# Graph layers computed as A(xW) in place of (Ax)W, in a one-core graph, mixer and FFN block

## The reference

```
xn = layernorm(x)
g  = prelu(xn @ lin_W.T + lin_b)
for l in 0, 1:
    h = g + segment_sum(g[src], dst)                  # = A g, A = I + counts of edges
    h = prelu(h @ W1[l].T + b1[l], conv_a[l])
    h = h @ W2[l].T + b2[l]
    g = relu(batchnorm_over_nodes(h))
m  = linear attention mixer of xn (q softmax over 64, k softmax over nodes), projected, layernormed
x  = x + g + m
x  = x + ffn(layernorm(x))                            # weights merged from 8 experts by a gate
```

## Time and profile before

| what | value |
|---|---|
| median of 3 runs | 558.52 us |
| profiled execution | 561.2 us, of which 558.6 us from first to last instruction |
| busy | PE 496.5 us (89%), DVE 342.3 (61%), ACT 233.5 (42%), POOL 165.5 (30%) |
| chain that ended last | PE 65%, DVE 19%, ACT 7%, issue 5% |
| granted clock of PE, mean | 0.954 of full speed |

### The profile page before, as it was taken

The page is one execution under the profiler, slowest core; times in us unless marked ns, Lnnn a source line. Parts: engine busy times, 40 slices in busy tenths (PEclk is TensorE's granted clock), DMA queues, the critical chain, the costliest instruction groups (busy, mean ns, idle before and its releaser), DMA issues.

```text
span 558.6 us, 11588 instructions
## 1 busy us (share of the span) xinstructions
PE 496.5 (89%) x3909; PEld 389.9 (70%) x3909; DVE 342.3 (61%) x731; ACT 233.5 (42%) x533; POOL 165.5 (30%) x142
## 2 busy tenths in 40 slices
PE   2988599999889889999999988799999978989792
PEld 2776488766455756679988877599888857856541
DVE  4679888589798267555266543212675375537686
ACT  4744122553323422224255448211355377733343
POOL 1564400040860300024974610000446023304312
PEclk9998799999999899999999997899999957999997
DMA  8502200020200200020000010000210294000014
GB/s 247 164 2 75 76 1 3 1 75 1 77 0 1 78 1 1 1 79 0 0 1 0 11 66 1 3 1 0 82 48 0 79 412 191 2 0 2 0 54 129
DMA packets 5246, 27.45 MB, mean 49 GB/s; under 512 B 1036, under 2 KB 1161, under 8 KB 3544
## 3 DMA queue, kind: packets, MB, share of 16 engines
q1 hardware_dynamic: 5208, 26.92, 13.9%
HBM read 24.36 MB, written 2.56 MB: 48 GB/s over the span
## 4 chain that ended last, share of the span: by engine, by line
PE 65%; DVE 19%; ACT 7%; issue 5%; POOL 1%; DVEq 1%; DMA 1%; ACTq 0%; SPq 0%
PE ps L455 38%; PE ps L600 15%; PE ps L442 4%; PE ps L509 3%; PE ps L499 2%; DVE stage L1447 2%; DVE ohs L1078 1%; DVE r L1159 1%; DVE r L1087 1%; DVE late L1088 1%; PE ps L709 1%; PE ps L439 1%; ACT r L920 1%; DVE r L1517 1%; ACT late L837 1%
## 5 line engine op out<-in xcount | busy, mean ns | idle before, releaser
L455 PE MATMUL ps<-late,wslot 128*128 x960 | 104.7, 269 | 1.0 <-ACT ohs L894 0.9
L455 PE MATMUL ps<-r,wslot 128*128 128x250 f16 x840 | 99.8, 279 | 5.1 <-DVE r L1087 5.0
L455 PEld LDWEIGHTS ps<-late,wslot 128*128 128x128 f16 x960 | 92.3, 97 | 13.1 <-issue 3.5
L1578 POOL TENSOR_TENSOR wslot<-stage,wslot 128x2048 f16<-128x2048 f32 x9 | 36.8, 4086 | 206.4 <-ACT wslot L752 129.0
L455 PEld LDWEIGHTS ps<-r,wslot 128*128 128x128 f16 x840 | 84.3, 101 | 18.5 <-DVE r L1087 6.6
L600 PE MATMUL ps<-late,r 125*128 (+1 forms) x800 | 90.5, 274 | 4.9 <-issue 3.4
L600 PEld LDWEIGHTS ps<-late,r 125*128 125x128 f16 x800 | 78.6, 99 | 15.1 <-issue 6.0
L455 PE MATMUL ps<-wslot,r 128*125 128x512 f16 x300 | 71.3, 387 | 2.6 <-DVE late L1088 2.6
L1088 DVE SCALAR_TENSOR_TENSOR late<-ps,late 128x250 f32 (+2 forms) x60 | 29.1, 502 | 61.2 <-ACT late L927 55.6
L455 PEld LDWEIGHTS ps<-wslot,r 128*125 128x125 f16 (+1 forms) x300 | 39.5, 138 | 26.5 <-DVE late L1088 4.0
L759 ACT ACTIVATE late<-ps 125x500 f16<-125x500 f32 (+1 forms) x25 | 14.7, 588 | 100.6 <-PE ps L442 100.6
(11 more groups left out here) (174 smaller groups left out, 697.2 us busy)
## 6 DMA issues: line engine op xcount, KB each, us to landing
late<-in_tv SPq DMA_DIRECT2D x2, 4096.0 KB, 17.4
x<-in_x SPq DMA_DIRECT2D x5, 448.0 KB
out<-r SPq DMA_DIRECT2D x10, 224.0 KB
stage<-in_w_up SPq DMA_DIRECT2D x2, 1024.0 KB, 5.1
stage<-in_w_down SPq DMA_DIRECT2D x2, 1024.0 KB, 4.9
stage<-in_w_lin SPq DMA_DIRECT2D x1, 1024.0 KB, 6.8
stage<-in_w_k SPq DMA_DIRECT2D x1, 1024.0 KB, 6.1
stage<-in_w_q SPq DMA_DIRECT2D x1, 1024.0 KB, 4.7
```

Source lines behind the costliest of these rows:

```text
L455: last = nc.tensor.matmul(out, stat_(hs, b), mov(hm, b), start=start and n == 0, stop=stop and n == 3 * blocks - 1)
L1578: nc.gpsimd.tensor_tensor(wslot[:, i % SLOTS, 1].rearrange("p k n -> p (k n)"), stage[:, :], wslot[:, i % SLOTS, 0].rearrange("p k n -> p ...
```

## The change

Since A(g W1) = (A g) W1, the first weight is applied before the gather. A natural product ("up0", "up1": `up_tile`) with the transposed features `in_t` as stationary operand gives u = g W1 in rows, which is what the gather takes as its stationary operand. So:

- the 80 flips of features to rows (`x0`, `x1`) and the transposed products up0 and up1 go; 10 natural tiles of 12 matmuls with 512 columns come in for each layer: those of layer 0 between the linear and the key stage, those of layer 1 in the ramp in which the flips were;
- the PSUM of the gather is taken up with the bias and goes straight to the PReLU; `high_sums` and `low_sums` go; the high and low parts of the features are made before the product (layer 0: `high_in`, `low_in` in the linear stage; layer 1: `high_in1` with the ReLU on ACT, `low_in1` on DVE);
- windows: one for each of the tiles 5 to 9 of up0, one a chunk in the key stage, the value stage as before, one for each of the first five mixer tiles; the check of the counts is moved into the last mixer tiles and `first_sums` goes; DVE loads five window columns at a time;
- weights: ACT scales them and writes the high part, POOL only the low part, and DVE's high parts go, but for lin and up0, which DVE and ACT make in the linear stage;
- the mixer's layernorm on ACT and POOL is spread over gather 0 and down0; loops of ACT, DVE and POOL there are unrolled; buffers change places (`gnn_t` in r2, x2 in r3, index preparation in `late`).

The core of the diff:

```diff
-WEIGHTS = ["lin", "k", "q", "v", "out", "up0", "down0", "up1", "down1", "gate"]
+WEIGHTS = ["lin", "up0", "k", "q", "v", "out", "down0", "up1", "down1", "gate"]
-WINDOWS = {"k": 2, "v": 2, "mix": 1}
+WINDOWS = {"up0": 1, "k": 1, "v": 2, "mix": 1}
+UP_LAG, FIRSTS_AT = 5, 2
 # PE
+            def up_tile(layer, t):
+                def ready(b):
+                    if t % 2 == 0:
+                        pe.wait_ge(in_low, KB * (J * layer + t // 2) + b + 1)
+                wait_bank(pe, "x", f"up{layer}", t, t % 2)
+                passes(bank("x", t % 2)[0:P, :], lambda h, b: in_t[:, h, b, t * P:(t + 1) * P],
+                       lambda h, b: weight(f"up{layer}")[:, h, b, :], KB, ready=ready).then_inc(full["x"], 1)
+            wait_weight(pe, "up0")
+            for t in range(T):
+                up_tile(0, t)
...
+                if t >= UP_LAG:
+                    windows("up0", t - UP_LAG)
-                    if m % 2 == 0:
-                        pe.wait_ge(lin_out, KB * j + KB)
-                        flip_tile_to_nat("x", "x0", gnn_t, 2 * j + m // 2)
-                if t:
-                    windows("mix", (t - 1) // 2, (t - 1) % 2, 2)
-            windows("mix", HT - 1, 1, 2)
+                if 1 <= t <= J:
+                    windows("mix", t - 1)
+                if t == T - 3:
+                    pe.wait_ge(chk_ready, 1)
+                    nc.tensor.matmul(ps[0:1, 6, 0:2], ones[0:P, 0:1], chk[:, 0:2], start=True, stop=True).then_inc(chk_sum, 1)
...
-            first_sums((0, 1))
...
+                    wait_weight(pe, "up1")
                     for t in range(T + 2):
                         if t < T:
-                            flip_tile_to_nat("x", "x1", gnn_t, t, lambda m: pe.wait_ge(layer_out, KB * (t // 2) + m + 1))
+                            up_tile(1, t)
                         if t >= 2:
-                            wait_done(pe, "x", "x1", t - 1)
+                            wait_done(pe, "x", "up1", t - 1)
...
-                transposed(f"up{layer}", weight(f"up{layer}"), h_t,
-                           ready=lambda j: wait_done(pe, "t", f"agg{layer}", KB * j + KB))
 # ACT
+            def scale_weight(name):
...
+                nc.scalar.activation(stage[:, :], stage[:, :], ACT.Copy, scale=S_W).then_inc(w_scaled, 1)
+            def high_in(j, blocks):
...
+                for m in blocks:
+                    act.wait_ge(lin_out, KB * j + m + 1)
+                    nc.scalar.activation(in_t[:, 0, m, chunk], lin_t[:, m, chunk], ACT.Copy).then_inc(in_high, 1)
             for j in range(J):
                 lin_blocks(j, (0, 1))
+                if j:
+                    high_in(j - 1, (2, 3))
...
                 lin_blocks(j, (2, 3))
+                high_in(j, (0, 1))
+                if j == 1:
+                    high_weight("up0", S_W)
...
-            split_weight("up0")
+            split_weight("down0")
 # DVE
+            def low_in1(j):
...
+                for m in range(KB):
...
+                    nc.vector.tensor_scalar(shifted[:, m, :], gnn_t[:, m, chunk], bn_scale[:, m:m + 1], bn_shift[:, m:m + 1],
+                                            ALU.mult, ALU.add).then_inc(bn_out, 1)
+                for m in range(KB):
+                    dve.wait_ge(in_high, KB * (J + j) + m + 1)
+                    nc.vector.scalar_tensor_tensor(in_t[:, 1, m, chunk], shifted[:, m, :], 0.0, in_t[:, 0, m, chunk],
+                                                   ALU.max, ALU.subtract).then_inc(in_low, 1)
-                low_sums(0, slice(0, CH))
...
 # POOL
-                nc.gpsimd.tensor_scalar(stage[:, :], stage[:, :], S_W, 1.0, ALU.mult, ALU.mult).then_inc(w_scaled, 1)
+            for j in range(J):
+                low_prelu(0, j)
+                if j == J - 2:
+                    mix_tile(0)
+                    mix_tile(1)
```

More of the change, by code:

```diff
@@ L635, in _, with gather @@
                                      ).then_inc(g_full, 1)
-            def gather(phase, general, first_done):
+            def gather(layer, general):
                 def chunk_sums(j, chunk, tiles):
@@ L875, in _ @@
                     high_tile_t("qt", q_t, t + 4, S_Q)
-                windows("mix", t // 2, t % 2, 2)
-            split_weight("down0")
+                if t < J:
+                    windows("mix", t)
+                if t in (2, 6):
+                    scale_weight("up1" if t == 2 else "down1")
+                if t in (3, 7):
+                    high_weight("up1" if t == 3 else "down1")
             act.wait_ge(rare_ready, 1)
@@ L1051, in then, with first_columns, windows @@
                 dve.wait_ge(dve_step, steps[0])
-            def first_column(w):
-                return dve.value_load(window_at[0:1, w:w + 1], min_val=0, max_val=COLS)
             column = []
-            def windows(phase, i, part, parts):
+            def first_columns(w):
+                _, at = nc.values_load_multi_w_load_instructions(
+                    window_at[0:1, w:min(w + AT_ONCE, NWIN)], engines=[mybir.EngineType.DVE], min_val=0, max_val=COLS,
+                    skip_runtime_bounds_check_because="a count of at most COLS heads, less one, and not below zero")
+                column.extend(at)
+            def windows(phase, i, part=0, parts=1):
                 for w, slot in window_list(phase, i, part, parts):
-                    at = column.pop() if column else first_column(w)
+                    at = column[w]
                     dve.wait_ge(adj_full, w + 1)
@@ new lines, in _ @@
+            for layer in range(L):
+                for j in range(J):
+                    for m in range(0, KB, 2):
+                        prelu_pair(layer, j, m)
+                        if layer == 0 and j < 2:
+                            for t in ((0, 1), (2, 3, 4), (5, 6), (7, 8, 9))[2 * j + m // 2]:
+                                last = nc.vector.bn_stats(stat[0:P, 6 * t:6 * t + 6], mix_nat[:, t, :])
+                    if layer == 0 and j == 1:
+                        then(last)
+                        aggregate(0, T)
+                    if layer == 0 and j == 2:
+                        normalizer(0, T, TURN["mix"])
```

453 lines of the change are left out of this document (242 added, 211 removed).

## The result

| | before | after |
|---|---|---|
| median of the runs, us | 559.0 (4 runs) | 569.2 (4 runs, 566.5 to 571.9) |
| ratio, 95% interval | 1 | 1.0173 (1.0148 to 1.0199) |
| profiled execution, us (span) | 561.2 (558.6) | 566.5 (564.6) |
| instructions on PE, busy | 3909, 496.5 us | 3589, 492.2 us |
| chain: PE, DVE, issue | 65%, 19%, 5% | 67%, 17%, 5% |

The forecast was 554.8 us, with a range of 544.5 to 562.5. The change is 1.7% slower, outside that range.

The account below looks back on a forecast made before the run. The prediction took the kernel as PE-bound with places where PE waits. Its terms, 1.5 - 9.9 + 3.5 + 3.8 + 2.0 - 4.6 = -3.7 us, taken off 558.5, gave 554.8 us, range 544.5 to 562.5.

Parts of the forecast that it names:

- up0 and key stage: From up0 through the key products: 81.0 us before, 71.1 after with tiles, products, windows and three waits; -9.9 us.
- After that the stage has room: up0 and key stage, beyond three counted waits: a window takes DVE 2.5 us and a low part 0.7, against PE's 3.9.
- Other meetings: POOL's weight passes meeting DVE's windows: q's in the key stage 2.5 us, up1's in the mixer stage 1.0; +3.5 us.
- Weights on ACT: Query and value stage: ACT's one more pass of 1.89 us each for v and out delays PE uncovered; +3.8 us.
- Check and branch: Ahead of the first gather: with nothing covering the check, PE has a gap of 2.2 to 3.4 us; +2.0 us.
- Linear stage: Start of the kernel: added ACT and DVE work makes chunks late, and the stage ends at 52.3, not 50.8; +1.5 us.
- ramp: Ramp into layer 1 with up1 and its gather: 87.6 us before, 83.0 after, PE starting 5.6 us in; -4.6 us.
- The rivals: Whole kernel: counted waits don't come, 543.4 us (0.20); POOL's passes hold windows, 564.1 (0.20); ramp gives nothing, 559.4 (0.10).
- Rival 2: POOL's passes for k, q, up1 and down1 each hold a one-hot pass and PE waits; 564.1 us, chance 0.20.

Follow-up runs that it names:

- dve_early: The changed kernel with DVE building each key window two products earlier, PE's order untouched; 554.8 us, ratio 0.9896.
- pool_tiny: The changed kernel with POOL's low-part passes for q and down1 cut from 2048 to 16 columns; 562.9 us, ratio 1.0054.
- self_early: The changed kernel with the last diagonal addition put ahead of the check, beside the other nine; 569.1 us, ratio 1.0151.
- combo_k: dve_early plus later up0 windows on PE, ACT's v and out passes moved earlier, POOL's k pass earlier, all diagonal additions ahead of the check; 540.5 us, ratio 0.9643.
- dve_one: The changed kernel with DVE building each key window one product earlier, PE's order untouched; 557.7 us, ratio 0.9951.

## Why the prediction was wrong

**up0 and key stage, -9.9 us, was +7.3: the step that failed.** Its products, tiles and windows were sized right: dve_early's key stage is 33.0 us where they give 33.3. In up0 the waits were near the forecast too: none at tile 2, 1.44 us for the first window's offsets, 1.76 beside k's pass, and 38.9 us for the stage where the terms give 37.8. What failed is the sentence "After that the stage has room", since a window and a low part take DVE 3.2 us against 3.9 of PE. That compares rates, and for up0's tiles; for the keys, where PE has 2.6 us, I worked out nothing and set the 2.6 only against the meeting with q's pass. What decides is the time from the event at which DVE's queue lets a window begin to PE's turn for it, against DVE's steps to the offsets (0.5 + 1.4) and PE's load of them (1.1, which I had not looked for): 2.6 against 3.0 us in the key stage. The trace of before had it: late, the first window's matmuls took 2.29 us, in time 1.10, and I booked the first as a wait alone. I also took the flips off PE and didn't ask what their 0.51 us had covered. The 49.4 us of the stage are 33.0 (dve_early), 7.7 for five late windows (pool_tiny less dve_early), and 8.7 for the meeting with q's pass and the slow clock behind it (after less pool_tiny).

**Other meetings, +3.5.** For q I took 2.5; it was the largest single event, 4.26 us of wait and 8.7 with the clock. The 2.6 us of cover that I counted against it were already spent on the window's own 3.0, so all of the pass came through (4.26 us against 0.42 in pool_tiny), and I had left out the clock. For up1 I took 1.0, and it didn't come: the pass began at 256.32 us, as DVE finished a window. The mixer stage fell by 2.3. I didn't list down1's pass as a meeting in the sum at all; beside it the last addition took 2.05 us. The rule that I weighed, in the Trainium skill, SBUF — State Buffer, section Who interferes with whom, is borne out again, and more sharply: a 1x16 instruction took 4.02 us beside GpSimd's pass, so the price is the pass's length (4.07 us where nothing met it) and not the size of the blocked work.

**Weights on ACT, +3.8, was +4.4: the waits were right, the number in after is in part luck.** The wait at the value tile grew from 1.68 to 3.62 us, by 1.94 for one pass of 1.90. The one ahead of a flip of k grew from 0.86 to 2.64 in dve_early, but only to 1.00 in after, where PE came out of the late last key window with a slow clock (36 matmuls in 9.64 us, against 7.96 in dve_early). With other waits gone, PE's idle time in the stage rose by some 0.6 us only; the rest is the same 451 matmuls at a clock of 0.94 in place of 1.00, 75.3 us busy against 71.5. Moved away, both waits went.

**Check and branch, +2.0, was +5.3.** The gap was 4.83 us and not 2.2 to 3.4, with down1's pass on GpSimd beside the last addition, which I had not counted; without one or the other it is 3.06 (pool_tiny) and 2.79 (self_early), inside the forecast. The gather behind it ran at a clock of 0.93.

**Linear stage, +1.5, was -1.2; ramp, -4.6, was -5.8.** Chunk 3 began at 38.06 us (38.8 forecast), chunk 4 at 44.48 (47.0): DVE caught up between the chunks, which my walk had it not do (0.28 us of idle ahead of chunk 4). But the -1.2 is luck of the clock. The same wait stands ahead of chunk 3 in all twelve traces, and behind it the same 36 matmuls took 4.01 us in five of them and 5.31 to 6.88 in seven; after, then dve_early:

```profile
38.06 4.01 PE L458 MATMUL ps<-r,wslot 128*128 128x250 f16 x36 [3.63 <-DVE r L1133]
...
38.84 6.88 PE L458 MATMUL ps<-r,wslot 128*128 128x250 f16 x36 [3.62 <-DVE r L1133]
```

With it the stage is 49.4 to 53.3 us long, -1.4 to +2.5, which has the forecast's +1.5 in it. The ramp's 5.88 us of idle ahead of up1 are the 5.6 forecast. The order A(xW) itself does what it was to do: the flips went and the ramp gave its time.

**The rivals.** Rival 2 had the right sign and, with GpSimd's passes, half of the mechanism; it gave 564.1. None of the three named a window that is late by DVE's own order, so the range had no room for it. Two of its four meetings, k's and q's, held PE for long, down1's lengthened the gap, and up1's fell between two windows.

## What to carry to other kernels

Check a hand-over by its latency, not by the two engines' rates: from the event that lets the producer start, through each of its steps and the consumer's own preparation, to the consumer's turn; when you take work off the consumer or thin out what stood in between, work this slack out anew for each place. A small shortfall is not small: five windows late by 0.39 to 1.7 us cost 7.7 us here, and a meeting that added 3.8 us of idle cost 8.7 with the clock behind it. And place a GpSimd pass over a whole weight where no DVE step is on a path; a table of who meets whom is worth as much as the sum of the durations.

## What the hardware showed that I had not expected

- Sixteen matmuls of 80 columns at addresses loaded at run time took 0.75 to 0.88 us behind queued 512-column matmuls, 1.1 to 1.2 behind 24 or more 250-column ones, and 1.8 to 2.3 behind idle time of 0.2 us or more; by the number of windows under 0.95 us, up to 1.4, and over, after has 14, 0 and 11 and combo_k 15, 5 and 5. Four of combo_k's last five, of 1.52 to 1.73 us, stand behind no idle time, so lateness is not the only thing that slows them. At fixed columns they took 0.75 behind 250-column products.
- The load of 16 addresses took PE's sequencer 1.10 us in the median of 25, and 1.30 at most.
- The holding goes both ways. The GpSimd pass that stretched DVE's offsets shows 4.84 us where 4.07 is usual: it began at 93.28, while DVE's one-hot pass ran to 94.20, and DVE's next instruction then ended with it, at 98.14. In dve_one it began 0.02 us behind a one-hot pass and shows 4.74; DVE's pass kept its 0.83, and its evacuations from PSUM meanwhile their 0.42.
- Around the stall of 4.26 us the granted clock was 0.84 (93.0 to 99.8 us), then 0.50, which is the 1.2 GHz level, for the window behind it (99.8 to 101.6), and 0.79 to 108.6; 48 matmuls took 6.70 us where they take 5.28 at 1.00. The clock behind a wait differs between executions: behind 3.62 us in the linear stage dve_early shows 0.52 (40 to 45 us) and after 1.00. No run here shows what decides it.
